# One exp per PSUM bank instead of one over two banks, and a wait per bank, in the four attention layers of head depth 8

## What is computed

```
scores = einsum('bqhd,bkhd->bhqk', q, k) * scale      # 16 heads, depth 8
attn   = softmax(scores, axis=-1)                     # exp, then sums over k
out    = einsum('bhqk,bkhd->bqhd', attn, v)           # then out @ wo, residual, norm
```

## Time and profile before

| what | value |
|---|---|
| median of 3 runs | 382.58 us (382.28 to 383.41) |
| profiled execution | 382.29 us |
| its span in the trace | 380.6 us |
| TensorE busy | 336.4 us, 88% |
| VectorE busy | 241.7 us, 64% |
| ScalarE busy | 200.9 us, 53% |
| exps of the depth-8 layers (line 381) | 64: 48 of 1025 ns, 16 of 1114 ns |

### The profile page before, as it was taken

The page is one execution under the profiler, slowest core; times in us unless marked ns, Lnnn a source line. Parts: engine busy times, 40 slices in busy tenths (PEclk is TensorE's granted clock), DMA queues, the critical chain, the costliest instruction groups (busy, mean ns, idle before and its releaser), DMA issues.

```text
span 380.6 us, 9089 instructions
## 1 busy us (share of the span) xinstructions
PE 336.4 (88%) x3621; PEld 212.6 (56%) x3621; DVE 241.7 (64%) x458; ACT 200.9 (53%) x419; POOL 90.8 (24%) x254
## 2 busy tenths in 40 slices
PE   4779998997989989998898999979999998999981
PEld 1334445665778778867543444445455665565550
DVE  6524366527986666859647778788565446546834
ACT  1345656647686668676523435344555534445550
POOL 7114242300300001003045113413413304313311
PEclk9999999999999999999999999999999999999997
DMA  7266000000000000000000000001000000000000
GB/s 229 95 232 255 0 3 3 2 2 0 2 0 3 2 2 0 2 2 28 29 0 22 36 29 28 16 3 43 22 30 10 2 14 16 2 16 9 22 15 29
DMA packets 7450, 11.94 MB, mean 31 GB/s; under 512 B 2024, under 2 KB 4464, under 8 KB 7152
## 3 DMA queue, kind: packets, MB, share of 16 engines
q1 hardware_dynamic: 6720, 10.04, 7.6%
q10 hardware_dynamic: 688, 1.32, 0.9%
HBM read 6.63 MB, written 0.52 MB: 19 GB/s over the span
## 4 chain that ended last, share of the span: by engine, by line
PE 67%; ACT 14%; DVE 10%; issue 5%; DMA 2%; POOL 1%; POOLq 0%; ACTq 0%; SPq 0%
PE psum L275 16%; PE psum L330 7%; PE psum L655 4%; PE psum L304 4%; PE psum L284 4%; PE psum L680 4%; PE psum L714 4%; ACT probs L381 3%; PE psum L566 3%; ACT probs L756 3%; PE psum L706 3%; ACT probs L764 3%; PE psum L631 3%; PE psum L691 2%; PE psum L874 2%
## 5 line engine op out<-in xcount | busy, mean ns | idle before, releaser
L452 DVE TENSOR_REDUCE maxs<-psum 128x8 f32<-128x1024 f32 x64 | 78.1, 1222 | 67.4 <-PE psum L265 28.1
L275 PE MATMUL psum<-km,qT 32*128 32x512 f32 x256 | 71.0, 634 | 17.6 <-ACT v1all L636 3.8
L381 ACT ACTIVATE probs<-psum 128x1024 f32<-128x1024 f32 x48 | 49.2, 1025 | 51.2 <-PE psum L304 49.8
L284 PE MATMUL psum<-qm,kT 32*128 32x512 f32 x256 | 72.1, 638 | 0.7 <-ACT probs L381 0.7
L275 PEld LDWEIGHTS psum<-km,qT 32*128 32x128 f32 x256 | 20.0, 183 | 31.7 <-issue 26.7
L330 PE MATMUL psum<-probs,vpad 128*32 128x128 f32 x1024 | 34.5, 275 | 2.1 <-DVE probs L462 2.1
L756 ACT ACTIVATE probs<-psum,maxs 128x128 f32<-128x128 f32 x128 | 34.9, 392 | 0.5 <-DVE maxs L804 0.5
L524 POOL TENSOR_SCALAR rstd<-stats 128x2 f32<-128x2 f32 (+1 forms) x18 | 6.7, 372 | 116.1 <-DVE stats L488 116.1
L330 PEld LDWEIGHTS psum<-probs,vpad 128*32 128x32 f32 x1024 | 26.2, 109 | 13.2 <-DVE probs L462 5.1
L431 POOL CAST mp<-maxs 128x16 bf16<-128x16 f32 x32 | 6.8, 214 | 98.3 <-DVE maxs L452 98.2
L304 PEld LDWEIGHTS psum<-mrow,sel 32*128 32x128 bf16 x512 | 17.4, 93 | 19.8 <-issue 18.2
(11 more groups left out here) (151 smaller groups left out, 622.6 us busy)
## 6 DMA issues: line engine op xcount, KB each, us to landing
km<-kT SPq DMA_DIRECT2D x30, 64.0 KB, 1.9
wmat<-in_wmat SPq DMA_DIRECT2D x1, 1856.0 KB, 13.2
qm<-qT SPq DMA_DIRECT2D x16, 64.0 KB, 1.9
wmat<-in_wmat SPq DMA_DIRECT2D x1, 1024.0 KB, 8.9
qm<-qT SPq DMA_DIRECT2D x32, 32.0 KB, 1.8
wrow<-in_wrow SPq DMA_DIRECT2D x1, 704.0 KB, 5.4
ctxT<-in_ctxt SPq DMA_DIRECT2D x2, 256.0 KB, 4.8
xnT<-in_xt ACTq DMA_DIRECT2D x2, 256.0 KB, 6.5
```

The costliest lines, as they stand in the source:

```text
L275: s_mm = e.matmul(bank(j), qT[rg(j), bt(b)], km[L.slot][rg(j), :, bt(b)], start=True, stop=L in (LC, L3), skip_group_check=True)
L284: e.matmul(bank(4 + a), kT[rg(j), M.slot, bt(b)], qm[rg(j), :, bt(b)], start=True, stop=False, skip_group_check=True)
L381: e.activation(probs_of(n, half), bank(4, 2), ACT.Exp, bias=masked, scale=layer(n).scale)\
L452: e.tensor_reduce(maxs[:, n % 2, 8 * half:8 * half + 8], bank(2 * half, 2).rearrange("p (h k) -> p h k", k=P), AX.X, ALU.max, negate=True)\
```

## The change

The exp over banks 4 and 5 becomes two exps of 512 columns, one for each bank, and each raises `exp_done`. The wait in `T_ready` is gone; each of the two T matmuls now waits for its own bank's exp of the half before. The other waits on `exp_done` count in the new unit and mean what they meant. The first exp still waits for `T_mm`, which the last of the eight line-304 matmuls raises for both banks.

```
@@ T_ready
             if n == 0 and half == 0:
                 e.wait_ge(*L0.past("v_out", 1))
                 e.wait_ge(*L0.past("k_out", 2))
-            if 2 * n + half:
-                e.wait_ge(sem("exp_done"), 2 * n + half)
@@ pe_scores
                 T_ready(e, m, mhalf)
                 for a in range(2):
                     j = 2 * mhalf + a
+                    if 2 * m + mhalf:
+                        e.wait_ge(sem("exp_done"), 4 * m + 2 * mhalf - 1 + a)
                     e.matmul(bank(4 + a), kT[rg(j), M.slot, bt(b)], qm[rg(j), :, bt(b)], start=True, stop=False,
                              skip_group_check=True)
@@ pe_V
-                e.wait_ge(sem("exp_done"), 2 * n + 2)
+                e.wait_ge(sem("exp_done"), 4 * n + 4)
@@ act_exp
-            e.activation(probs_of(n, half), bank(4, 2), ACT.Exp, bias=masked, scale=layer(n).scale)\
-             .then_inc(sem("exp_done"), 1)
+            for a in range(2):
+                e.activation(probs_of(n, half)[:, a * HALF:(a + 1) * HALF], bank(4 + a), ACT.Exp, bias=masked, scale=layer(n).scale)\
+                 .then_inc(sem("exp_done"), 1)
@@ dve_past
-            e.wait_ge(sem("exp_done"), 2 * n + half + 1)
+            e.wait_ge(sem("exp_done"), 4 * n + 2 * half + 2)
@@ block.tensor, after the steps of L0
-            e.wait_ge(sem("exp_done"), 2 * B)
+            e.wait_ge(sem("exp_done"), 4 * B)
```

## The result

The changed kernel takes 383.97 us (median of 9 runs, 383.37 to 385.23), the kernel before 382.58 us (9 runs, 382.19 to 383.93): a ratio of 1.0034, 95% interval 1.0018 to 1.0049. It is slower by 1.4 us, between 0.7 and 1.9. On a second chip it was 384.05 against 382.63 us, ratio 1.0035 (1.0011 to 1.0060). The forecast was 384.7 us: the right side, the right mechanism, and 0.7 us too much of it.

A forecast was written before the change was run, and what follows sets the result against it. TensorE, 88% busy, was taken to bound the kernel, with ScalarE on 14% of the chain. Losses of 1.1 + 0.5 + 0.45 = 2.1 us on 382.29 gave 384.4, or 384.7 us as a median; range 382.2 to 387.0 us.

The forecast's parts named there:

- What bounds: TensorE 88% busy; T waits 3.3 us for exps, while S waits 9.5 us for ScalarE's copies, many standing behind an exp.
- ScalarE, two exps for one: On ScalarE, each second exp ends later: 0.16 us for L0's 16 exps, 0.075 us for the other 48.
- Copies behind exps in L0: Seven exps on L0's chain are followed by a copy TensorE waits for: 7 x 0.16 = 1.1 us lost.
- Copies without a bias column: After L0, seven exps without a bias column are followed by such a copy: 7 x 0.075 = 0.5 us lost.
- T by bank: At waiting T's the first matmul starts 0.4 us earlier, but the pair ends 0.075 later: 6 x 0.075 = 0.45 us lost.
- The third rival: T by bank pays at 7 waits: 3.2 us gained, 1.6 of copies lost, about 381.1 us; chance 0.11.
- Extra waits at nothing: On TensorE, 56 more waits with the semaphore already up cost nothing; at 0.01 us each, 0.6 us.
- Rivals 1 and 2: 1: whole fixed part shows, slower by 3 to 4.4 us, chance 0.10; 2: it is absorbed, 382.6 to 383.5 us, 0.17.
- Sum: Copies in L0, later copies and waiting T's together: 1.1 + 0.5 + 0.45 = 2.1 us slower.

The follow-up runs named there:

- e6: Four exps of 256 columns for each half, a T matmul waiting for the second or the fourth; 7.5 us slower than the kernel before by the medians.
- e10: The kernel before with only the two waits ahead of an exp swapped (V_mm first, then T_mm); 1.9 us slower by the medians.
- e1: The change with its two exps, but one wait for both ahead of both T matmuls; 384.38 us, +1.9 against the kernel before.
- e4: The change in L2, LC and L3 alone, one exp elsewhere with a wait per T matmul; +1.0 us over the kernel before by the medians.
- e2: The kernel before with one exp kept, but a wait of its own ahead of each T matmul; 0.1 us by the medians.
- e11: The kernel before with S_ready waiting first for the copy that frees its bank; 378.82 us, ratio 0.9906.
- e5: The change plus the eight small matmuls by bank, the first exp waiting for bank 4 alone; 2.8 us slower than the kernel before.
- e8: As e5, but the exp waits for the small matmuls ahead of V_mm; +1.4 us over the kernel before.

## Why the prediction was right, point by point

- **What bounds.** Right. The place that the change hurts is S behind a copy behind an exp, the place that it helps is T. S's three waits grew by 1.2 us, T's shrank by 0.8.
- **ScalarE, two exps for one.** Taken 0.16 and 0.075 us for each further instruction; measured 0.15 (1.26 less 1.11) and 0.06 (1.08 less 1.02), and linear up to four. The second exp starts 0.49 and 0.59 us behind the first and the copy 0.97 and 1.15, forecast 0.50, 0.58, 1.00 and about 1.20. ScalarE's busy time grew by 4.3 us, not 6. The Trainium skill ("ScalarE: Activation LUTs", section "What ACT_TABLE_LOAD costs") had given 0.187 and 0.093 us, as an estimate from its fixed parts and overlap. This kernel shows less, and the measurement decides.
- **Copies behind exps in L0: the term that was mis-sized.** "7 x 0.16 = 1.1 us" measured 0.83 us. At five of the seven places the step is 0.10, not 0.15. The copy started 1.05 us after the exp at these places and 1.01 at the two others. I read both as ScalarE's spacing. At the five, it was TensorE's own matmul for V1 that ended last: in the kernel before it ends at 33.45 + 1.13 = 34.58 and the copy starts at 34.61, so the copy had some 0.05 us of cover.

```profile
33.45 1.13 PE L631 MATMUL psum<-wmat,ctxT 128*128 128x512 f32 x2
```

  In the change the copy starts 1.15 us after the exp at these places:

```profile
33.72 1.26 ACT L382 ACTIVATE probs<-psum,mu 128x512 f32<-128x512 f32 x2
34.87 0.58 ACT L637 COPY v1all<-psum 128x512 f32<-128x512 f32 x1
```

  e6 agrees: its step of 0.41 us is three further instructions of 0.15 less the same 0.05. So does e10: its exps are 0.06 us later, and at the places with that cover the step is at most 0.02, at the other two 0.06.
- **Copies without a bias column.** "7 x 0.075 = 0.5 us" put the price at 0.075, and the step is 0.06: the copy of qT starts 0.97 us after the exps, 0.92 before, and S behind it 0.06 us later. But S was late behind a copy at nine places, not seven: at 330.08 and 345.42 us as well, which were not on the chain of the kernel before.

```profile
270.55 1.08 ACT L382 ACTIVATE probs<-psum 128x512 f32<-128x512 f32 x2
271.52 0.48 ACT L580 ACTIVATE qT<-psum,bcol 128x256 f32<-128x256 f32 x1
```

- **T by bank.** Right in kind: the first matmul 0.4 us earlier, the second 0.06 later. The third rival, a pair served in turn, is out: the exp starts 1.38 us behind the second matmul, whether the first started with it (277.50, exp at 278.89) or 0.48 us ahead of it (278.61, exp at 280.00). "6 x 0.075 = 0.45 us" was too much: four T's left a step of 0.06 (those at 198.65, 277.50, 354.05 and 364.73 us), those at 217.69 and 233.59 us none, and the one at 359.44 us gave back 0.04, because of its waits and not of its bank (e1). The prediction had left out the one at 233.59, as it should, but had taken seven of the eight waits of the earlier trace rows for waits that an exp ends. They are six: at 361.99 and 367.27 us T starts 0.14 us after the exp's end, at the six others 0.05, so at those two something else ended last. The rule on rotating through banks (the Trainium skill, "Perfetto Trace Analysis", section "Matmuls") brought nothing here (e1 and e4); the reading that fits the trace is that both banks of a half are filled at the same time by two row groups.
- **Extra waits at nothing.** Right (e2).
- **Rivals 1 and 2.** The overhead shows at its smaller size, so rival 1 is out. A little is absorbed, at two T's and by the cover in L0, but not half of it.
- **Sum.** 0.83 us in L0, less 0.05 in L1, and twelve steps of 0.06 behind it (nine copies, three T's) make 1.5 us of drift to 360 us; the T's at 359.44 and 364.73 us add 0.01. By the medians it is 1.4, and 2.1 was forecast. That thirteen places behind L0 were forecast (seven copies, six T's) and thirteen steps came (nine and four) is luck; what made the forecast too large is the price of each, 0.16 for 0.10 or 0.15 and 0.075 for 0.06.

## What to carry to other kernels

Cutting an instruction in two to let a consumer start on the first part pays only if that part's work is not done beside the second part's anyway; here the two matmuls ran in different row groups, so only the end of the last one counted, and that came later. Price a further instruction by the spacing of neighbours in the trace, not by its fixed duration, and look for what stands behind it on its own engine: the S matmuls paid, which the change did not touch. Where an instruction has several waits, write the one that ends last first: that gained 3.4 us, over twice what the change lost.

## What the runs showed that I had not expected

- The order in which waits are written matters. The first is carried by the instruction and answered in 0.04 us; one that stands later becomes a record of its own and costs 0.06 us more at an exp (e10) and 0.09 us more at a matmul (e11).
- TensorE starts matmuls of another row group before older ones are over, but in e5 their semaphore came only when the older one had ended (280.65 against 280.38 us), and so in e8 (281.17 against 280.90).
- In some runs the granted clock of the span is 0.987 to 0.990 instead of 0.991 to 0.996, and the time 1 to 2 us longer. A trace of e4 shows the place: by stretches (us; busy time and count of PE, PEld, DVE, ACT, POOL; then the clock), TensorE ran at its lower level, 1.2 GHz, for most of 203 to 206 us, after it had stood idle for 1.35 us, ahead of an S that starts at 203.41. The idle time alone does not decide it: at the same S TensorE stood idle for 1.29 us in the kernel before and for 1.35 in the changed one, and both kept 2.4 GHz in their traces.

```profile
195.00:200.00 5.00, 4.51 (x33) 2.05 (x31) 2.87 (x9) 1.35 (x3) 2.85 (x6) 1.00 0.00 0
200.00:203.00 3.00, 2.06 (x18) 0.85 (x15) 2.08 (x3) 1.75 (x4) 2.92 (x6) 1.00 0.00 0
203.00:206.00 3.00, 2.59 (x10) 0.68 (x10) 2.22 (x2) 0.27 (x1) 0.90 (x2) 0.54 0.02 5
```

  In a few runs it is 0.972 to 0.984 and the time 2.5 to 5 us longer. The trace of e10 is one of these (0.977): its drift is 0.87 us at 360 us, but its span is 4.4 us longer, and TensorE ran at 1.2 GHz through the stretch from 370 to 380 us, where the mean in the kernel before is 0.81.

```profile
370.00:380.00 10.00, 6.95 (x54) 4.27 (x50) 4.46 (x17) 1.93 (x4) 1.27 (x4) 0.50 0.03 8
```

  In 5 of the 35 runs of the kernel before on one chip and in 5 of the 12 of e4 beside them the clock was at or under 0.989. Whether these 0.06 us of longer exps make the fall more likely is open: the counts are small and nothing was tried on it.
